# Two of the opening weight pieces loaded by a second queue and rounded by VectorE, in a Strassen feed-forward kernel

## What is computed

```python
W = weights[condition]                              # 128 indices, 16 matrices of 64 x 64
y = jnp.einsum('bct,bcd->bdt', x, W)
result = jnp.einsum('bnd,od->bno', y, W_base) + b_base
probs = softmax(jnp.einsum('bnd,ed->bne', y, W_gate))
top_p, top_i = jax.lax.top_k(probs, 2)              # two of eight experts
route_w = jnp.sum(one_hot(top_i, 8) * (top_p / sum(top_p))[..., None], axis=-2)
h = jnp.einsum('bnd,erd->bner', y, A)               # rank 16 for each expert
delta = jnp.einsum('bner,eor->bno', h * route_w[..., None], B)
return x + result + delta
```

## Time and profile before

| | |
|---|---|
| median of 3 runs | 939.24 us |
| the profiled execution: its own time | 939.58 us |
| the profiled execution: span | 937.6 us |
| TensorE busy | 931.8 us, 99% |
| VectorE / ScalarE / GpSimd busy | 657.8 / 380.6 / 515.5 us |
| all DMA | 107.13 MB, mean 114 GB/s |

### The profile page before, as it was taken

The page is one execution under the profiler, slowest core; times in us unless marked ns, Lnnn a source line. Parts: engine busy times, 40 slices in busy tenths (PEclk is TensorE's granted clock), DMA queues, the critical chain, the costliest instruction groups (busy, mean ns, idle before and its releaser), DMA issues.

```text
span 937.6 us, 17680 instructions
## 1 busy us (share of the span) xinstructions
PE 931.8 (99%) x5415; PEld 880.2 (94%) x5415; DVE 657.8 (70%) x2274; ACT 380.6 (41%) x812; POOL 515.5 (55%) x506
## 2 busy tenths in 40 slices
PE   8999999999999999999999999999999999999998
PEld 7999999999999999999999999999999999999998
DVE  5787667676677776776766767667767667676675
ACT  6553443443434433434334344343443443433432
POOL 2566555655556545566455565455654556655550
PEclk9999999999999999999999999999999999999999
DMA  9523333223333233232233332333323324223312
GB/s 310 186 79 103 133 108 116 101 89 123 113 110 120 72 121 134 89 127 93 103 125 112 112 103 87 123 120 104 123 79 112 134 92 131 91 99 123 112 68 90
DMA packets 41484, 107.13 MB, mean 114 GB/s; under 512 B 4481, under 2 KB 8706, under 8 KB 41474
## 3 DMA queue, kind: packets, MB, share of 16 engines
q1 hardware_dynamic: 41472, 107.01, 33.5%
q10 hardware_dynamic: 2, 0.00, 0.0%
HBM read 73.43 MB, written 33.55 MB: 114 GB/s over the span
## 4 chain that ended last, share of the span: by engine, by line
PE 99%; DMA 0%; ACT 0%; DVE 0%; SPq 0%; issue 0%; DVEq 0%
PE ps L846 54%; PE ps_r L846 19%; PE ps_out L864 11%; PE ps_out L874 9%; PE ps L905 3%; PE ps L916 1%; PE ps_r L905 1%; DMA r_raw<-in_w_t 0%; PE ps_r L916 0%; PE ps L891 0%; PE ps_r L891 0%; PE ps L864 0%; PE ps L874 0%; ACT r_hi L435 0%; PE ps_hwt L870 0%; DVE o_sb L675 0%
## 5 line engine op out<-in xcount | busy, mean ns | idle before, releaser
L325 POOL TENSOR_TENSOR a_lo<-raw,a_hi 128x512 fp32r<-128x512 f32 x128 | 168.4, 1328 | 154.1 <-ACT a_hi L427 152.0
L665 DVE STREAM_TRANSPOSE ps_hwt<-hw 32x32 f32<-32x32 f32 x944 | 210.4, 223 | 29.6
L846 PE MATMUL ps<-w_hi,s_hi 128*128 128x448 f32 x480 | 176.0, 367 | 0.0
L846 PE MATMUL ps<-w_lo,s_hi 128*128 128x448 f32 x480 | 174.1, 363 | 0.0
L846 PE MATMUL ps<-w_hi,s_lo 128*128 128x448 f32 x480 | 173.8, 362 | 0.0
L846 PE MATMUL ps_r<-r_lo,a_hi 128*128 128x264 f32 x496 | 141.3, 285 | 0.0
L846 PE MATMUL ps_r<-r_hi,a_hi 128*128 128x264 f32 x496 | 140.8, 284 | 0.0
L846 PE MATMUL ps_r<-r_hi,a_lo 128*128 128x264 f32 x496 | 140.8, 284 | 0.0
L846 PE MATMUL ps<-w_hi,a_hi 128*128 128x448 f32 x360 | 131.4, 365 | 0.0
L846 PE MATMUL ps<-w_hi,a_lo 128*128 128x448 f32 x360 | 131.1, 364 | 0.0
L846 PE MATMUL ps<-w_lo,a_hi 128*128 128x448 f32 x360 | 130.7, 363 | 0.0
(11 more groups left out here) (137 smaller groups left out, 1699.7 us busy)
## 6 DMA issues: line engine op xcount, KB each, us to landing
raw<-in_x_t SPq DMA_DIRECT2D x128, 256.0 KB, 2.8
o_sb<-in_x SPq DMA_DIRECT2D x64, 512.0 KB, 3.7
out_x<-o_sb SPq DMA_DIRECT2D x62, 512.0 KB, 2.6
w_sum<-in_w_t SPq DMA_DIRECT2D x6, 448.0 KB, 10.2
r_raw<-in_w_t SPq DMA_DIRECT2D x4, 264.0 KB, 5.4
w_sum<-in_w_t SPq DMA_DIRECT2D x4, 224.0 KB, 5.2
table_raw<-in_cond_w SPq DMA_DIRECT2D x2, 256.0 KB, 8.8
b_raw<-in_b_t SPq DMA_DIRECT2D x1, 512.0 KB, 10.0
```

Source lines behind the costliest of these rows:

```text
L325: pool.tensor_tensor(a_lo[j][:], raw[j][:], as_f32(a_hi[j][:]), ALU.subtract).then_inc(s_a_lo[j], 1)
L665: dve.transpose(ps_hwt[c * TURN:(c + 1) * TURN, r * TURN:(r + 1) * TURN], hw[r * TURN:(r + 1) * TURN, c * TURN:(c + 1) * TURN]).then_inc(s ...
L846: mm = pe.matmul(bank[:, 0:w.shape[-1]], a[:, k, :], w[:, k, :], start=(opens and k == 0 and q == 0), stop=(closes and k == KH - 1 and q = ...
```

## The change

The loads of R pieces 0 and 1 move from SyncE's queue to ScalarE's, where they are the first instructions. The load of the indices, which stood there, moves to SyncE, behind B21 and ahead of the table. VectorE makes the tops of these two pieces, each just ahead of its rest, counted by a semaphore of their own (`s_r01_hi`), and TensorE waits on that one. ScalarE's two `r_top` calls go. The warm-up has eight matmuls.

```diff
-WARM_UP = 10
+WARM_UP = 8
...
             load_raw(0, A11)
-            load_r(0)
             load_raw(0, A21)
-            load_r(1)
             for k in range(KH):
                 load_b11(k)
...
             load_w("B21")
+            sp.dma_start(cond_sb[:], cond).then_inc(s_cond_in, 16)
...
-            act.dma_start(cond_sb[:], cond).then_inc(s_cond_in, 16)
+            for j in range(2):
+                act.dma_start(r_raw[:, ks(j), :], w_t.rearrange("(k p) n -> p k n", p=P)[:, ks(j), cols(R)])\
+                    .then_inc(s_r_in[j], 16)
...
             a_top(0, A11)
-            r_top(0)
             a_top(0, A21)
-            r_top(1)
...
+            def r_top(j):
+                dve.wait_ge(s_r_in[j], 16)
+                dve.tensor_copy(r_hi[:, ks(j), :], r_raw[:, ks(j), :]).then_inc(s_r01_hi, 1)
+
             def r_rest(j):
-                dve.wait_ge(s_r_hi, j + 1)
+                if j < 2:
+                    dve.wait_ge(s_r01_hi, j + 1)
+                else:
+                    dve.wait_ge(s_r_hi, j - 1)
...
             for j in range(2):
+                r_top(j)
                 r_rest(j)
...
-            pe.wait_ge(s_r_hi, 1)
+            pe.wait_ge(s_r01_hi, 1)
             r_kind(0, 0, HH)
...
-            pe.wait_ge(s_r_hi, 2)
+            pe.wait_ge(s_r01_hi, 2)
```

## The result

The changed kernel is slower, by less than I had called measurable: 941.24 us median (20 runs, 940.45 to 941.86) against 939.50 us for the kernel before (20 runs, 938.56 to 941.61), a ratio of 1.0017 with a 95% interval of 1.0011 to 1.0023. I had forecast 938.7 us and a range up to 939.7 us. The profiled execution took 941.25 us, span 939.4 us, against 939.58 and 937.6 us.

What follows compares the result with a forecast made beforehand. TensorE bounds the kernel, and only its opening can gain. Load -0.47 us, top -0.04 us and 0 for indices, warm-up and ScalarE's head make -0.5 us: 938.7 us against the median 939.24 us, range 937.9 to 939.7 us.

Steps and rivals of the forecast that it cites:

- What bounds the kernel now: TensorE runs without a gap from 6.60 us; only the opening can gain, at most 2.4 us.
- R 0's load: Issued earlier on ScalarE's queue, landing at 5.33 us: 0.47 us gained, bounds 1.2 us gained to 0.5 us lost.
- The top on VectorE: R 0's copy takes 0.60 us against ScalarE's 0.64 us: -0.04 us, range -0.3 to +0.5 us.
- R 1 behind it: R 1 lands at 6.3 us, needed by 7.0 us; landing as before would hold the gain to 0.25 us.
- Eight warm-up matmuls: In the opening, dropping two matmuls behind the clock's rise is worth nothing on the path.
- (c): Clock rises later than 4.2 us in some executions, real work starts at half rate: 940.2 us, chance 0.04.
- (a): DMA engines, not the issue, bound R's landing; nothing moves (within 0.25 us): 939.2 us, chance 0.22.
- (b): R 0's packets alternate with those of A21 and B11, so R 0 lands behind A21: 939.7 us, chance 0.12.
- (d): Two queues fill the early DMA stretch and VectorE's copy is fast: 938.0 us, chance 0.20.
- The indices' load: Issued on SyncE behind B21, first used by GpSimd just ahead of 24.58 us: costs nothing.
- ScalarE's head: Second issue shifts the table load from 1.35 to about 1.8 us; cover 0.15 us ahead of A11's top, costs 0.
- B21's cover: B21's rest is done 0.60 us before TensorE comes at 18.79 us; gain exceeding that could become a wait.

Runs made afterwards that it cites:

- e2: Kernel before with only the tops of R pieces 0 and 1 moved to VectorE: 939.62 us, ratio 1.0008.
- e4: Kernel before with only the warm-up cut to eight matmuls: 939.41 us, ratio 1.0007.
- e12: Kernel before with twelve warm-up matmuls: 939.06 us, ratio 1.0000.
- e7: Changed kernel with the tops of R pieces 0 and 1 on ScalarE and ten warm-up matmuls: 938.93 us, ratio 0.9996.
- e11: Changed kernel with tops on ScalarE and ten warm-up matmuls, repeated on another chip: 939.00 us, ratio 1.0000.
- e6: Changed kernel with five more matmuls on zeros among the first R matmuls: 941.83 us, ratio 1.0024.
- e8: Changed kernel with R 1's top on ScalarE and ten warm-up matmuls: 939.39 us, ratio 1.0006.
- e1: Changed kernel with the tops of R pieces 0 and 1 back on ScalarE, eight warm-up matmuls kept: 938.99 us, ratio 1.0002.
- e3: Changed kernel with ten warm-up matmuls: 940.13 us, ratio 1.0011.
- e5: Changed kernel with GpSimd's subtractions for A11 and A21 of the first pair cut to one element: 939.83 us, ratio 1.0000.
- e9: Changed kernel with GpSimd's A11 and A21 subtractions of the first pair left out and ten warm-up matmuls: 938.53 us, ratio 0.9995.

## Why the prediction was wrong, point by point

**What bounds the kernel now** held: only the opening changed anything, and its shift is the span's. But I took R 0's landing at 5.80 us for typical. In three more profiles with the old order of loads (e2, e4, e12) it landed at 4.54, 4.41 and 4.56 us, and R 1 at 6.4 to 6.6 instead of 7.2 us. The single execution I read was a late one for these loads (its span of 937.6 us is in the upper third of the kernel before, too). In the other three, R 0 was there earlier than the 5.33 us that the new queue was to give.

**R 0's load** landed at 4.92 us, inside my bounds (5.33 forecast); with the new order it is 3.9 to 4.4 us from issue in ten profiles, so 4.7 to 5.2 us: later than in those three. R 1, at 6.5 to 6.8 us in eight of them, gained nothing on those three either. What I left out is A11, which I had called far ahead: sharing the engines with R 0 it lands 0.6 to 0.9 us later (3.2 to 3.5 instead of 2.6 us from issue), and with it moves GpSimd's subtraction of A11, from 4.16 - 5.42 us to 4.96 - 6.51 us, onto the rest of R 0. The line of the kernel before:

```profile
4.16 1.26 POOL L325 TENSOR_TENSOR a_lo<-raw,a_hi 128x512 fp32r<-128x512 f32 x1 [2.12 <-ACT a_hi L427]
```

So TensorE, starting earlier than before, found the rest of A11 missing and waited 0.56 us for it, 0.3 us of which are GpSimd's own wait behind the copy. My sum followed A11 only to its top and had no term for its rest. The rule that I cited from the Trainium skill's "DMA: Bandwidth & Descriptors", section "Issuing engines are not separate DMA queues", that only the issue time is saved, agrees with the landings and with e7 and e11 (0.9996 and 1.0000), whose intervals allow the 0.47 us as well as nothing.

**The top on VectorE** and **R 1 behind it** are the step that failed. I gave the copy 0.60 us, with up to 0.5 us more if GpSimd ran beside it, and used the 0.60 us for the second copy too, although the row I cited for GpSimd (7.19 us, 1.29 us long) lay right where that copy would stand. Alone it takes 0.43 us (the estimate from the Trainium skill's "VectorE: DVE Perf Modes", section "Mode 2×_2P — use both read ports for one tensor", was 0.28 us and some overhead, which leaves 0.15 us for that); behind GpSimd it took 1.16 to 1.54 us, and the subtraction 1.67 us instead of 0.71. The price isn't a slower rate but a wait for GpSimd's instruction to end. Whatever its start, a caught copy ended 0.29 to 0.30 us behind GpSimd's end (e2, e6, e8 and the changed kernel) and a caught subtraction 0.55 to 0.57 us behind it (e1, e3, e4 and the changed kernel). The 1.14 us of the earlier trace rows was already that wait, 8.48 us (end of GpSimd's) plus 0.57. The Trainium skill's "SBUF — State Buffer", section "SBUF: two separate sides", states it: the port pair that VectorE and GpSimd share is an exclusive lock held for the whole instruction, for copies in a two-port mode and operations with two inputs in SBUF. e5 and e8 agree, 0.43 against 1.54 us. GpSimd's 1.55 us behind the copy against 1.26 agrees as well: the wait goes both ways. I had cited that skill for the copy's speed and not asked what the speed takes. R 1's top came at 8.51 us, where by my own sum TensorE needed it by 7.6 us (its landing, at 6.6 us, was in time); held up by A11's rest, TensorE came for it at 8.12 us and still waited 0.44 us. So the term that I had at -0.04 us, the tops on VectorE, was a loss, as e1 and e5 show: 0.9 us by e3's lowest span against e7's, 1.2 us against e9's, which leaves GpSimd's subtractions out altogether.

**Eight warm-up matmuls** I costed at nothing, on one execution in which the rise came at 4.2 us. Read from the matmuls' spacing, it came anywhere from 4.0 (e9) to 10.4 us (e6) in my profiles. With eight matmuls, 5 of 11 (e4), 4 of 11 (e1) and 7 of 11 (e5) runs had a span of 937.8 us or more; with ten and the tops on ScalarE or GpSimd's subtractions away, 10 of 99 (before) and none of 33 (e7, e9, e11). e5 against e9 and e1 against e7 and e11 differ in the two matmuls alone, but ran on different chips; e4 against the kernel before is on one chip and weaker (5 of 11 against 5 of 33, and from 938.2 us up 5 against 2). Ten do not help everywhere: where the copies wait for GpSimd (e3, e8) 3 and 5 of 11 were in an upper group. So rival (c) was the right place, with 0.04 far too small a chance, and its price of 1.5 us fits (the upper groups of e1 and e5 lie 0.9 to 2.1 us above the lower). But it had only the late rise. In the changed kernel's own profile the clock had risen in time, two R matmuls taking 0.48 us at 5.52 us, and fell again at 8.0 us: no term and no rival had that. A slip beside it: the zeros ended 1.1 us, not 0.9 us, ahead of the 6.1 us at which I had the first real matmul.

**The two together.** The three waits split TensorE's work from 4.8 to 8.6 us, and the clock falls again later. The mean clock of 0.998, the sign of such a fall, came in 14 of 20 runs of the changed kernel and 4 of 11 on another chip. With ten warm-up matmuls (e3), with the tops alone (e2) and with the short warm-up alone (e4) it came in 1 of 11 each, in e1 and e5 in none. So the falls are frequent only where both are there; that is what the counts show. That the pauses are what brings the fall is argued: the fillers meant to prove it settled nothing, and why 14 of 20 in one set and 4 of 11 in another stays open. In size, e3 has 0.85 us over its kernel before by the medians, and the changed kernel 1.74 us: so roughly half are the waits and half the clock.

**Rivals.** (a) was near the truth for the loads. (b) came half true: the loads do share the engines, but A11 paid, not R 0. (d) fell, though its fast copy came true. R 0's landing, the one sign by which I would have called the prediction wrong, stayed inside its 4.6 to 5.9 us, and the first matmul came earlier than forecast (5.52 us). What caught the loss was another of my signs, no other wait of TensorE behind the first: there were two. The indices' load, ScalarE's head (A11's top now waits 0.94 us for its data) and B21's cover cost nothing, as said: TensorE has no wait there in any profile.

## What to carry to other kernels

Before an operation is moved to VectorE, look at what GpSimd does at that time: a float32 copy or a two-input operation in SBUF waited here for the rest of GpSimd's instruction and took 0.3 us (the copy) or 0.57 us (the subtraction) behind it, and ScalarE paid nothing of that kind (0.63 us beside GpSimd in e1). Before a warm-up is shortened, time it in many runs, since one profile shows one of many times at which the clock can rise (4.0 to 10.4 us here). And where a gain is a few tenths of a microsecond from one landing, ask a second execution for that landing first.

## What the runs showed that I had not expected

The granted clock's column reads 1.00 from the start up to the first fall, so half rate ahead of the first rise is seen only in the matmuls' spacing: 0.22 us for 264 columns, 0.43 us for 512. A copy that starts 0.03 us ahead of GpSimd took 0.43 us, one 0.01 us behind it 1.54 us. With the second queue in use the first block landed 0.6 to 0.9 us later at the same size.
